# A macaron block with a sorted mixture of experts: each row block is loaded and transposed once and kept, and ScalarE copies each tile's operand from the kept block

## The chip, the cores and the metric

The kernel runs on one core of a Trainium2 chip. The metric is the device time of one launch in microseconds (us). Before the change three runs gave 845.37, 845.60 and 845.91 us, median 845.6 us.

## The reference, cut to what matters

The input x has 4 batches of 512 rows of 256 f32 values. The block adds half a mixture of experts, then a causal attention, then half of the same mixture of experts again, each on the layer norm of x:

```python
x = x + 0.5 * _L0_ffn_ref(_layernorm(x), router_w, gate_w, up_w, down_w)
x = x + _L0_attn_ref(_layernorm(x), Wqkv, Wo)
x = x + 0.5 * _L0_ffn_ref(_layernorm(x), router_w, gate_w, up_w, down_w)

# _L0_ffn_ref: E = 16 experts, K = 2 of them for each row, F = 96, D = 256
probs = softmax(x @ router_w)
routing_weights, routing_idx = top_k(probs, 2)   # weights divided by their sum
expert_out = (silu(x @ gate_w[e]) * (x @ up_w[e])) @ down_w[e]
out = sum over a row's two experts of weight * expert_out
```

The attention has 16 query heads and 4 key heads of 128 values, with rotary embedding.

## The kernel before, in words

**Pools and visits.** A mixture of experts is done by sorting. GpSimd (POOL) scatters each token's normalized row twice, once for each of its experts, with indirect DMAs into a DRAM buffer `xs`, where rows stand in the order of their experts. There are four pools: p0 (batch 0) and p1 (batches 1 to 3) for the first mixture, p2 (batches 0 to 2) and p3 (batch 3) for the second. A pool of `nt` row tiles has `nr = 2 nt` sorted blocks of 128 rows: 8 in p0 and p3, 24 in p1 and p2. Since the boundary between two experts may fall inside a block, a block is multiplied with each expert that has rows in it. This gives `ns = nr + 15` visits (the code calls them tiles): 23 in p0 and p3, 39 in p1 and p2, 124 in all. Visit s belongs to expert e = `tab[s]` and to block s - e. The table is worked out on the chip, so an engine that needs e reads it into a register (TENSOR_LOAD).

**A step of a visit.** `steps(n)` runs over the visits of mixture n, and each engine's program is written out by hand in that order, software-pipelined. At the step of visit `at`:
- SP loads the block of a later visit from `xs` (`load_tile`, a ring of 10 places) after a register read, and stores the output of an earlier one in `ys` (`store_tile`).
- TensorE (PE) runs `gate_up(at)` (two 128x192 matmuls, whose stationary operand is the transposed block in `sb_xT`), `tile_transposes(at + 2)` (two 128x128 transposes of a loaded block into one of two PSUM banks), `load_expert(at + 1)` (the register read), `down(at - 2)` (two matmuls with `sb_hT` stationary), `h_transpose(at - 1)`, and whatever work of the routing or of the attention's projection lies beside.
- ScalarE (ACT) runs `silu(at)`, `xt_copy(at + 2)` (PSUM to `sb_xT`, two places) and `h_copy(at - 1)`.
- VectorE (DVE) runs `h(at)` and `evacuate(at - 2)` (PSUM to an output ring; in the first mixture it is scaled by a row weight that was loaded as column 256 of the block). Routing and norms lie beside.

Every block is so loaded and transposed once for each visit, 124 times. What a matmul needs is handed over by semaphores: `xg_in` (a load landed), `xt_ps` (a transpose is in PSUM), `xt_done` (`sb_xT` is written), `h_done`, `ht_done`, `y_ps` and `y_evac` (an output is evacuated).

**Around the stages.** In the first mixture the steps of p1 follow those of p0 without a break, while ScalarE and VectorE also split the attention's weights. The last steps of p1 carry the norm and projections of the attention. In the second mixture the first visits of p2 start inside the end of the attention, and p3's routing is done beside the first 23 steps of p2. The end is the gather of p3's outputs. Line numbers in the trace: `gate_up` and `down` L1698, `tile_transposes` L1757, `h_transpose` L1771, `silu` L930, `xt_copy` L926, `h` L1263, `evacuate` L1270 and L1272.

## Time and profile before

| | |
|---|---|
| median of three runs | 845.6 us |
| the profiled execution | 844.34 us, of it 842.5 us from the first to the last instruction (the span) |
| mean granted clock of TensorE | 0.978 of 2.4 GHz |
| busy: PE, DVE, ACT, POOL | 91%, 76%, 69%, 53% of the span |
| first mixture, first to last visit | 40.5 to 151.1 us |
| second mixture, first to last visit | 725.8 to 816.8 us |

The two mixtures take about 200 us of the span and the attention between them the rest. A visit is marked in the trace by its `silu`. Busy time counts the matrix work, not the waits; the stages with experts are read by stretches between such marks.

### The profile page before, as it was taken

To read this page: it belongs to the slowest core of one execution; us is meant where nothing else is said; L and a number is where in the kernel's file an instruction comes from. 1 tells how busy PE (TensorE), PEld (TensorE's weight loads), DVE (VectorE), ACT (ScalarE), POOL (GpSimd) and SP (SyncE) were. 2 spreads that over 40 slices of the span, in tenths; PEclk is the share of its full clock that TensorE was granted. 3 is DMA by queue.
4 is the path that set the end of the run, shared out by engine and by line. 5 is a ranking of instruction groups with operands and counts; after the bars stand their busy time and mean duration, and the time that the engine had idled before them with its cause. 6 is when DMAs were issued, how large, how long until landed. Compare 5 with 4: busy or idle time off the path is not lost.

```text
span 842.5 us, 16221 instructions
## 1 busy us (share of the span) xinstructions
PE 762.9 (91%) x4584; PEld 657.5 (78%) x4584; DVE 638.0 (76%) x1839; ACT 580.8 (69%) x1534; POOL 444.6 (53%) x382
## 2 busy tenths in 40 slices
PE   3698999799999999999999999999998989999980
PEld 3686788687878888888888888888887768789970
DVE  6565675578898888889988989997889858755572
ACT  2365657787877887878878787788776666556640
POOL 1571605587565775575667456364444783003374
PEclk9799999999999999999999999999999999999995
DMA  9497962121000100000010000000000156257785
GB/s 313 128 356 241 287 182 83 63 32 20 1 1 14 20 14 8 1 14 14 0 15 12 2 1 2 1 2 1 7 2 1 39 181 186 87 153 234 214 248 173
DMA packets 52918, 70.63 MB, mean 84 GB/s; under 512 B 7264, under 2 KB 44640, under 8 KB 52448
## 3 DMA queue, kind: packets, MB, share of 16 engines
q1 hardware_dynamic: 40736, 47.54, 18.1%
q0 software_dynamic: 9216, 16.82, 8.2%
q10 hardware_dynamic: 2880, 5.24, 1.9%
q8 instruction: 40, 0.66, 0.3%
q14 instruction: 46, 0.38, 0.1%
HBM read 42.80 MB, written 26.77 MB: 83 GB/s over the span
## 4 chain that ended last, share of the span: by engine, by line
PE 67%; DVE 8%; issue 8%; POOL 7%; DMA 4%; ACT 2%; SPq 1%; POOLq 0%; DVEq 0%; ACTq 0%
PE ps L1698 56%; PE ps L1904 6%; PE ps L1757 2%; POOL sb_xf L1647 2%; POOL sb_ropeB L1644 2%; DMA sb_wF_raw<-ys,sb_pos 1%; POOL xs L1605 1%; POOL xs L1613 1%; DVE sb_x L1480 1%; DMA sb_wF_raw<-xs 1%; PE ps L1771 1%; DVE sb_prob L1453 1%; PE ps L1718 1%; DVE sb_wF L1460 1%; PE ps L1865 1%
## 5 line engine op out<-in xcount | busy, mean ns | idle before, releaser
L1698 PE MATMUL ps<-sb_wF 128*128 128x512 f32 (+2 forms) x1056 | 260.2, 373 | 6.2 <-DVE sb_wF L1470 4.9
L1698 PEld LDWEIGHTS ps<-sb_wF 128*128 128x128 f32 x1056 | 171.8, 189 | 25.3 <-issue 5.4
L1698 PE MATMUL ps<-sb_wF,sb_wA 128*128 128x512 f32 x576 | 156.4, 407 | 10.6 <-ACT sb_ropeB L1004 10.0
L1644 POOL TENSOR_TENSOR sb_ropeB<-sb_ropeB,sb_sin 128x512 f32<-128x512 f32 x80 | 110.7, 1384 | 104.8 <-ACT sb_ropeB L1004 104.7
L1023 ACT ACTIVATE sb_prob<-sb_prob,sb_nmax 128x128 f32<-128x128 f32 (+3 forms) x256 | 142.1, 559 | 32.9 <-DVE sb_nmax L1453 32.2
L1655 POOL TENSOR_TENSOR sb_wF<-sb_xf,sb_wF 128x384 fp32r<-128x384 f32 (+1 forms) x75 | 82.3, 1105 | 115.2 <-ACT sb_wF L1016 115.0
L1480 DVE SCALAR_TENSOR_TENSOR sb_x<-ps,sb_rinv,sb_x 128x256 f32<-128x256 f32 x256 | 122.5, 479 | 20.1 <-PE ps L1698 8.9
L1698 PEld LDWEIGHTS ps<-sb_wF,sb_wA 128*128 128x128 f32 x576 | 102.9, 190 | 36.9 <-ACT sb_ropeB L1004 18.1
L1032 ACT ACTIVATE sb_wF<-ps 128x512 fp32r<-128x512 f32 x160 | 95.2, 595 | 43.4 <-PE ps L1904 42.8
L1460 DVE TENSOR_TENSOR sb_wF<-ps,sb_wF 128x512 fp32r<-128x512 f32 x160 | 109.2, 683 | 20.5 <-ACT sb_wF L1032 19.2
L1698 PE MATMUL ps<-sb_wA,sb_wF 128*128 128x256 f32 x768 | 115.5, 286 | 3.9 <-DVE sb_x L1480 3.3
L1698 PEld LDWEIGHTS ps<-sb_wA,sb_wF 128*128 128x128 f32 x768 | 104.1, 189 | 15.2 <-issue 8.3
L1647 POOL TENSOR_TENSOR sb_xf<-sb_xf,sb_ropeB 128x512 f32<-128x512 f32 x80 | 104.5, 1306 | 6.3
L1904 PE MATMUL ps<-sb_ident,sb_prob 128*128 128x128 f32 x640 | 94.0, 273 | 2.5 <-DVE sb_LC L1219 1.4
L1904 PEld LDWEIGHTS ps<-sb_ident,sb_prob 128*128 128x128 f32 x640 | 77.3, 140 | 18.4 <-issue 2.3
L1453 DVE CUSTOM_DVE_ANT_1 sb_prob<-ps,sb_wF_mask 128x384 f32<-128x384 f32 (+1 forms) x128 | 77.5, 618 | 9.4 <-PE ps L1698 8.9
L1698 PE MATMUL ps<-sb_wF_raw,sb_hT 96*128 (+1 forms) x248 | 76.4, 389 | 5.6 <-issue 2.5
L1263 DVE TENSOR_TENSOR sb_sg<-sb_sg,ps 128x96 f32<-128x96 f32 x124 | 31.3, 253 | 59.0 <-ACT sb_sg L930 57.9
L1003 ACT ACTIVATE sb_ropeB<-ps 64x512 f32<-64x512 f32 x80 | 47.6, 595 | 26.0 <-DVE sb_xf L1430 24.4
L1430 DVE SCALAR_TENSOR_TENSOR sb_xf<-ps,sb_cos 128x512 f32<-128x512 f32 x80 | 54.8, 685 | 13.4 <-PE ps L1698 6.7
L1635 POOL DMA_INDIRECT sb_x<-ys,sb_pos x32 | 50.8, 1587 | 26.6 <-DMA ys<-sb_wA_raw 20.5
L930 ACT ACTIVATE sb_sg<-ps 128x96 f32<-128x96 f32 x124 | 30.7, 248 | 45.5 <-PE ps L1698 45.4
(177 smaller groups left out, 1263.1 us busy)
## 6 DMA issues: line engine op xcount, KB each, us to landing
ys<-sb_wA_raw SPq DMA_DIRECT2D x124, 128.0 KB, 3.5
sb_wF_raw<-xs SPq DMA_DIRECT2D x44, 128.5 KB, 4.0
sb_wA_raw<-xs SPq DMA_DIRECT2D x44, 128.5 KB, 2.8
sb_work<-xs SPq DMA_DIRECT2D x36, 128.5 KB
sb_wA_raw<-in_wattn ACTq DMA_DIRECT2D x18, 256.0 KB, 4.4
sb_wF_raw<-in_wgu SPq DMA_DIRECT2D x4, 768.0 KB, 9.8
sb_wF_raw<-in_wdn SPq DMA_DIRECT2D x4, 768.0 KB, 11.6
sb_wA_raw<-in_wgu SPq DMA_DIRECT2D x4, 768.0 KB, 7.6
```

Source lines behind the costliest of these rows:

```text
L1023: nc.scalar.activation(own, own, ACT.Exp, scale=-1.0, bias=nmax[:, k % 2, h:h + 1], accum_out=ssum[:, k % 2, h:h + 1]).then_inc(exp_done, 1)
L1032: nc.scalar.activation(pT_at(tb, 0), ps[:, TBANK + tb % 2], ACT.Copy).then_inc(pt_hi, 1)
L1430: nc.vector.scalar_tensor_tensor(xf[:, rope_slot(col)], ps[:, bank], 1.0 if col == KCOL else SCALE, cos[:], ALU.mult, ALU.mult).then_inc(p ...
L1453: nc.vector.tensor_tensor_reduce(masked, scores, added, 1.0, TOP, ALU.add, ALU.min, nmax[:, k % 2, h:h + 1]).then_inc(nmax_done, 1)
L1460: nc.vector.tensor_tensor(pT_at(tb, 1), ps[:, TBANK + tb % 2], pT_at(tb, 0).bitcast(F32), ALU.subtract).then_inc(pt_lo, 1)
L1480: nc.vector.scalar_tensor_tensor(x[:, b, i], ps[:, wo_bank(b, k, h // 2), at:at + D], rinv[:, k % 4, h:h + 1], x[:, b, i], ALU.mult, ALU.a ...
L1635: nc.gpsimd.indirect_dma_start(out=x[:, t // T, t % T], out_offset=None, in_=ys[q.p][:], in_offset=where, compute_op=ALU.add).then_inc(acc ...
L1644: nc.gpsimd.tensor_tensor(ropeB[:, slot], ropeB[:, slot], sin[:], ALU.mult).then_inc(rope_mul, 1)
L1647: nc.gpsimd.tensor_tensor(xf[:, slot], xf[:, slot], ropeB[:, slot], ALU.add).then_inc(rope_sum, 1)
L1655: nc.gpsimd.tensor_tensor(lo[:, part], xf[:, rope_slot(col), part], hi[:, part].bitcast(F32), ALU.subtract)\
L1698: return nc.tensor.matmul(out, lhsT, rhs, start=start, stop=stop)
L1904: ins = nc.tensor.transpose(ps[:, TBANK + tb % 2, h * P:(h + 1) * P], prob[k % 2][:, h, j * P:(j + 1) * P], ident[:])
```

## The change

Each sorted block is loaded once by `load_block` (64 loads in place of 124; in the second mixture without the weight column, 256 in place of 257 values a row), into a ring of 6 places, and SP no longer reads a register. PE transposes it once (`turn`) into the same two PSUM banks. VectorE copies it from there into a kept region (`keep`; in the first mixture with a second copy of 128x1 for the weight column); only the first two blocks of p2 are kept by ScalarE, in the end of the attention. The semaphore `xt_kept` counts kept blocks. For each visit ScalarE copies the operand from the kept block into a ring of five places of `sb_xT` (`visit` takes the place of `xt_copy`). The block's address comes from a table that SP lays into one row by DMA (`table_row`) and that ScalarE reads four values at a time into registers. `turn(t)` waits until blocks up to t - 2 are kept, since they share the bank.

In mixture n = 0 each pool now runs its own steps from -2 to ns + 1, so p0 is finished before p1 begins. Block i + 4 is turned at step i and kept at step i + 1, so turns stand in steps 0 to 3 of p0, 0 to 19 of p1 and 0 to 19 of p2; p3's blocks are turned at steps 35 to 42 counted from p2's first. Query heads of a group are stored in reverse order, the DMA of a mask is issued later by SP, and the scatter waits for `xt_ps` to reach the new count of transposes.

```diff
+    TAB, TURNED = max(q.ns for q in pools), 5
...
-        xT = sb("xT", [P, 2, K * P], F32, own)
+        xT = sb("xT", [P, TURNED, D + 1], F32, own)
...
-    RING, XR, FR, GR = 8, 10, 4, 16
+    RING, XR, FR, GR = 8, 6, 4, 16
...
+    STARTS = {-2: (0, 1), -1: (2, 3)}, {0: (2, 3), 1: (4, 5)}
+    KEEPS = {-2: (0, 1), -1: (2, 3)}, {0: (2, 3), 2: (4, 5)}
+
+    def turned_blocks(q, at):
+        i = at - q.tiles if q.n == 0 else at - pools[2].tiles
+        out = [(q if q.n == 0 else pools[2], r) for r in STARTS[q.n].get(i, ())]
+        if q.n == 0 and 0 <= i and i + 4 < q.nr:
+            out.append((q, i + 4))
+        elif q.n == 1 and 2 <= i and i + 4 < pools[2].nr:
+            out.append((pools[2], i + 4))
+        elif q.n == 1 and 0 <= at + 4 - pools[3].tiles < pools[3].nr:
+            out.append((pools[3], at + 4 - pools[3].tiles))
+        return out
+
+    def kept_blocks(q, at):
+        i = at - q.tiles if q.n == 0 else at - pools[2].tiles
+        out = [(q if q.n == 0 else pools[2], r) for r in KEEPS[q.n].get(i, ())]
+        if q.n == 0 and 1 <= i and i + 3 < q.nr:
+            out.append((q, i + 3))
+        elif q.n == 1 and 3 <= i and i + 3 < pools[2].nr:
+            out.append((pools[2], i + 3))
+        elif q.n == 1 and 0 <= at + 3 - pools[3].tiles < pools[3].nr:
+            out.append((pools[3], at + 3 - pools[3].tiles))
+        return out
...
-        def load_tile(q, s):
...
+        def table_row(q):
+            sp.wait_ge(tab_done, q.p + 1)
+            sp.dma_start(row_tab[0:1, q.p % 2 * TAB:q.p % 2 * TAB + q.ns],
+                         tab[0:q.ns, q.p:q.p + 1]).then_inc(row_tab_in[q.p], 16)
+
+        def load_block(q, r):
+            t = q.at + r
+            if r == 0:
                 sp.wait_ge(scattered[q.p], 16 * q.nt * (1 if q.n == 0 else 2))
...
+            if t >= XR:
+                sp.wait_ge(xt_kept, t - XR + 1)
+            width = RW if q.n == 0 else D
+            sp.dma_start(block_rows(t)[:, 0:width], xs[q.p][r * P:(r + 1) * P, 0:width]).then_inc(xg_in[t % XR], 16)
...
-        def xt_copy(s):
-            act.wait_ge(xt_ps, s + 1)
-            nc.scalar.activation(xT[:, s % 2], x_at(s), ACT.Copy).then_inc(xt_done, 1)
...
+        def visit(q, s):
...
+            at = s - q.tiles
+            if at == 0:
+                act.wait_ge(row_tab_in[q.p], 16)
+            if at % 4 == 0:
+                more = min(4, q.ns - at)
+                own = row_tab[0:1, q.p % 2 * TAB + at:q.p % 2 * TAB + at + more]
...
+            act.wait_ge(xt_kept, q.at + min(at, q.nr - 1) + 1)
+            if s >= TURNED:
+                act.wait_ge(y_evac, s - TURNED + 1)
+            block = block_of_visit(q, at, visited[at % 4])
+            width = D + 1 if q.n == 0 else D
+            nc.scalar.activation(xT[:, s % TURNED, 0:width], block, ACT.Copy).then_inc(xt_done, 1)
...
-            nc.vector.tensor_scalar(yo(s), y_at(s), tile_at(q, s)[:, D:D + 1], None, ALU.mult).then_inc(y_evac, 1)
+            nc.vector.tensor_scalar(yo(s), y_at(s), xT[:, s % TURNED, D:D + 1], None, ALU.mult).then_inc(y_evac, 1)
+
+        def keep(q, r):
+            t = q.at + r
+            dve.wait_ge(xt_ps, t + 1)
+            ins = nc.vector.tensor_copy(kept_block(q, r, D), x_at(t))
+            if q.n == 0:
+                ins = nc.vector.tensor_copy(kept_block(q, r, RW)[:, D:RW], block_rows(t)[:, D:RW])
+            ins.then_inc(xt_kept, 1)
...
-                if has_tile(n, at - 2):
+                if has_tile(q, at - 2):
                     evacuate(pool_of(at - 2), at - 2)
-                if n == 0 and split_at(at - 1) is not None:
+                if not (q.p == 2 and i <= 2):
+                    for block in kept_blocks(q, at):
+                        keep(*block)
+                if n == 0 and has_tile(q, at) and split_at(at - 1) is not None:
                     weights_low(split_at(at - 1))
...
-        def tile_transposes(q, s):
-            pe.wait_ge(xg_in[s % XR], loaded(s))
+        def turn(q, r):
+            t = q.at + r
+            pe.wait_ge(xg_in[t % XR], loaded(t))
+            if t >= 2:
+                pe.wait_ge(xt_kept, t if t == pools[2].at + AHEAD else t - 1)
             for k in range(K):
-                ins = nc.tensor.transpose(x_at(s)[:, k * P:(k + 1) * P], tile_at(q, s)[:, k * P:(k + 1) * P], ident[:])
+                ins = nc.tensor.transpose(x_at(t)[:, k * P:(k + 1) * P], block_rows(t)[:, k * P:(k + 1) * P], ident[:])
             ins.then_inc(xt_ps, 1)
...
-                if has_tile(n, at + 2) and (n == 0 or i + 2 >= AHEAD or q.p == 3):
-                    tile_transposes(pool_of(at + 2), at + 2)
-                if has_tile(n, at) and has_tile(n, at + 1):
+                for block in turned_blocks(q, at):
+                    turn(*block)
+                if has_tile(q, at) and at + 1 < pools[2 * n + 1].end:
                     load_expert(at + 1)
```

PE, a step in the middle of p2, before: the second matmul of `gate_up`, the two transposes, the register read, `down` and `h_transpose` (an ISA row is the weight load with a register address that belongs to the matmul behind it).

```order
L1698 ISA
L1698 MATMUL ps<-sb_wA_raw,sb_xT 128x192
L1757 MATMUL ps<-sb_ident,sb_work 128x128 [waits xg_in9]
L1757 MATMUL ps<-sb_ident,sb_work 128x128
L1750 TENSOR_LOAD sb_tab
L1698 ISA [waits y_evac,ht_done]
L1698 MATMUL ps<-sb_wF_raw,sb_hT 128x256
L1771 MATMUL ps<-sb_ident,sb_sg 96x128 [waits h_done]
```

The same place after the change:

```order
L1817 ISA
L1817 MATMUL ps<-sb_wA_raw,sb_xT 128x192
L1879 MATMUL ps<-sb_ident,sb_work 128x128 [waits xt_kept,xg_in0]
L1879 MATMUL ps<-sb_ident,sb_work 128x128
L1869 TENSOR_LOAD sb_tab
L1817 ISA [waits y_evac,ht_done]
L1817 MATMUL ps<-sb_wF_raw,sb_hT 128x256
L1893 MATMUL ps<-sb_ident,sb_sg 96x128 [waits h_done]
```

The order is as it was, but the transpose now also waits on `xt_kept`, and behind it wait the register read, `down` and `h_transpose`. This stands in each step with a turn; in the other steps the two transposes are gone.

DVE, steps at the start of p2 while x is normalized beside them (L1153), before: `h`, `evacuate`, then other work.

```order
L1263 TENSOR_TENSOR sb_sg<-sb_sg,ps 128x96 [waits silu_done,stat_step]
L1270 COPY sb_wA_raw<-ps 128x256 [waits y_out0,y_ps]
L1153 TENSOR_SCALAR sb_wA_raw<-sb_x,sb_fmvO,sb_frsO 128x256 [waits wo_done]
L1153 TENSOR_SCALAR sb_wA_raw<-sb_x,sb_fmvO,sb_frsO 128x256
L1263 TENSOR_TENSOR sb_sg<-sb_sg,ps 128x96 [waits silu_done]
```

After the change the norm is L1258 and `keep` is L1382:

```order
L1368 TENSOR_TENSOR sb_sg<-sb_sg,ps 128x96 [waits silu_done]
L1375 COPY sb_wA_raw<-ps 128x256 [waits y_out1,y_ps]
L1382 COPY sb_wA_raw<-ps 128x256 [waits xt_ps]
L1258 TENSOR_SCALAR sb_wF_raw<-sb_x,sb_fmvO,sb_frsO 128x256 [waits wo_done]
L1258 TENSOR_SCALAR sb_wF_raw<-sb_x,sb_fmvO,sb_frsO 128x256
```

The copy into the kept region has come in behind `evacuate`, which itself waits on PE for `y_ps`.

ACT, the end of the attention and the first visit of p2, before: the last `xt_copy` of the two early blocks (L926), the load of the table of functions with a first use, and `silu`.

```order
L1038 ACTIVATE sb_wF<-ps 128x512 [waits wo_done,pv_done]
L926 ACTIVATE sb_xT<-ps 128x256 [waits xt_ps]
L1057 ACT_TABLE_LOAD
L1057 ACTIVATE sb_spare<-sb_exponent 128x1
L930 ACTIVATE sb_sg<-ps 128x96 [waits gu_done]
```

After the change:

```order
L1143 ACTIVATE sb_wF<-ps 128x512 [waits wo_done,pv_done]
L1030 ACTIVATE sb_wA_raw<-ps 128x256 [waits xt_ps]
L1162 ACT_TABLE_LOAD
L1162 ACTIVATE sb_spare<-sb_exponent 128x1
L1015 TENSOR_LOAD sb_row_tab [waits row_tab_in2]
L1025 ISA [waits y_evac,xt_kept]
L1025 ACTIVATE sb_xT<-sb_wA_raw 128x256
```

What was the operand's copy is now the `keep` of block 1 (L1030), and the operand of visit 0 is copied behind the load of the table, a register read and a wait.

## Rows read from the trace of the kernel before

**Rows 1.** The page: busy time, share of the span and instructions of each engine.
```profile
PE 762.9 (91%) x4584; PEld 657.5 (78%) x4584; DVE 638.0 (76%) x1839; ACT 580.8 (69%) x1534; POOL 444.6 (53%) x382
```

**Rows 2.** Windows of silu: stretch, length, busy (visits), PE clock, DMA share, GB/s.
```profile
77.87:111.72 33.85, 4.84 (x20) 1.00 0.96 269
111.72:151.30 39.58, 4.73 (x19) 1.00 0.36 108
725.80:732.05 6.25, 0.98 (x4) 1.00 0.07 22
732.05:758.78 26.73, 4.00 (x16) 1.00 0.53 158
758.78:785.73 26.95, 4.75 (x19) 1.00 0.75 226
785.73:817.10 31.37, 5.75 (x23) 1.00 0.82 241
```

**Rows 3.** Timeline, one plain step of p2: start us, us, engine, line, operation.
```profile
747.76 0.63 PEld L1698 LDWEIGHTS ps<-sb_wA_raw,sb_xT 128*128 128x128 f32 x4
...
747.87 0.81 PE L1698 MATMUL ps<-sb_wA_raw,sb_xT 128*128 x4
747.96 0.42 DVE L1270 COPY sb_wA_raw<-ps 128x256 f32<-128x256 f32 x1
...
748.30 0.26 DVE L1167 MAX8 sb_lgO<-ps 128x8 f32<-128x16 f32 x2
748.36 0.30 PEld L1757 LDWEIGHTS ps<-sb_ident,sb_work 128*128 128x128 f32 x2
...
748.63 0.30 PEld L1698 LDWEIGHTS ps<-sb_wF_raw,sb_hT 96*128 96x128 f32 x2
...
748.74 0.60 PE L1698 MATMUL ps<-sb_wF_raw,sb_hT 96*128 x2
...
748.96 0.12 PEld L1771 LDWEIGHTS ps<-sb_ident,sb_sg 128*96 128x96 f32 x1
```

**Rows 4.** Timeline of DVE in p1: an evacuation and the next operation.
```profile
96.68 0.48 DVE L1272 TENSOR_SCALAR sb_wA_raw<-ps,sb_wF_raw 128x256 f32<-128x256 f32 x1
...
97.08 0.68 DVE L1259 TENSOR_TENSOR sb_wA<-sb_wA_raw,sb_wA 128x512 fp32r<-128x512 f32 x1
```

**Rows 5.** Timeline of DVE: an operation on one column.
```profile
764.08 0.15 DVE L1245 TENSOR_SCALAR sb_tab<-sb_cntO 128x1 int32<-128x1 f32 x1
```

**Rows 6.** Timeline of DVE and the weight loads: end of h to its transpose.
```profile
729.32 0.23 DVE L1263 TENSOR_TENSOR sb_sg<-sb_sg,ps 128x96 f32<-128x96 f32 x1
...
729.61 0.12 PEld L1771 LDWEIGHTS ps<-sb_ident,sb_sg 128*96 128x96 f32 x1 [0.75 <-DVE sb_sg L1263]
```

**Rows 7.** Weight loads, start of p1: transposes that waited, and the next load.
```profile
74.31 0.20 PEld L1757 LDWEIGHTS ps<-sb_ident,sb_wF_raw 128*128 128x128 f32 x2 [1.82 <-DMA sb_wF_raw<-xs]
74.53 0.30 PEld L1698 LDWEIGHTS ps<-sb_wF_raw,sb_hT 96*128 96x128 f32 x2
...
78.72 0.20 PEld L1757 LDWEIGHTS ps<-sb_ident,sb_wF_raw 128*128 128x128 f32 x2 [1.15 <-DMA sb_wF_raw<-xs]
79.30 0.30 PEld L1698 LDWEIGHTS ps<-sb_wF_raw,sb_hT 96*128 96x128 f32 x2 [0.37 <-issue]
```

**Rows 8.** Timeline of PE, last two visits: from one h_transpose to the next.
```profile
815.79 0.27 PE L1771 MATMUL ps<-sb_ident,sb_sg 128*96 128x128 f32 x1
...
817.05 0.28 PE L1771 MATMUL ps<-sb_ident,sb_sg 128*96 128x128 f32 x1
```

**Rows 9.** Timeline, start of p2: first gate_up, table load, first silu.
```profile
724.12 0.63 PEld L1698 LDWEIGHTS ps<-sb_wA_raw,sb_xT 128*128 128x128 f32 x4
...
724.42 1.28 ACT L1057 ACT_TABLE_LOAD   x1
...
725.82 0.23 ACT L930 ACTIVATE sb_sg<-ps 128x96 f32<-128x96 f32 x1
```

**Rows 10.** Chain of work, 60 to 75 us: landing of the last scatter.
```profile
67.17 4.82 DMA xs<-sb_wF_raw,sb_toO
```

More of the change, by code:

```diff
@@ L34, in __init__ @@
         self.ns = self.nr + z.E - 1
-        self.end = tiles + self.ns
+        self.end, self.left = tiles + self.ns, at + self.nr
 class Sizes:
@@ L67, in program @@
         pools.append(Pool(z, len(pools), n, b0, b1, before.end if before else 0,
[L68 removed]
+                          before.halves + before.nh if before else 0, before.left if before else 0))
     MT = max(q.nt for q in pools)
     NFIRST = pools[1].end
+    TAB, TURNED = max(q.ns for q in pools), 5
     def sb(name, shape, dt, at=ctx):
@@ L207, in program @@
     xg_in = [sem(f"xg_in{r}") for r in range(XR)]
+    row_tab_in = [sem(f"row_tab_in{p}") for p in range(4)]
     xt_ps = sem("xt_ps")
+    xt_kept = sem("xt_kept")
     xt_done = sem("xt_done")
@@ L718, in steps @@
         first, second = pools[2 * n:2 * n + 2]
+        if n == 0:
+            for q in (first, second):
+                for i in range(-2, q.ns + 2):
+                    yield q, i, q.tiles + i
+            return
         for i in range(-2, first.ns + second.ns + 2):
@@ L826, in mask, with first_tiles, last_tiles @@
             sp.dma_start(mask_slots(n), A["mask"]).then_inc(mask_in[n], 16)
-        def tiles(first, second, then, at):
-            loads = [(first, s) for s in range(first.ns)] + [(second, s) for s in range(second.ns)]
-            out = 0
-            for m, (q, s) in enumerate(loads):
-                if m == at:
-                    then()
-                due = first.ns - RING if m == first.ns else m - XR + 1
-                while out < due:
-                    store_tile(*loads[out])
-                    out += 1
-                load_tile(q, s)
-            while out < len(loads):
-                store_tile(*loads[out])
-                out += 1
+        def first_tiles():
+            early, late = pools[0:2]
+            for r in range(early.nr):
+                load_block(early, r)
+            for i in range(2, early.ns + 2):
+                if i == 6:
+                    table_row(late)
+                store_tile(early, i - 2)
+                if i == early.ns - RING + 1:
+                    for r in range(XR):
+                        load_block(late, r)
+            for i in range(-2, late.ns + 2):
+                if i >= 2:
+                    store_tile(late, i - 2)
+                for q, r in kept_blocks(late, late.tiles + i):
+                    if r + XR < late.nr:
+                        load_block(late, r + XR)
+                if i == late.nr + E - 4:
+                    sp.wait_ge(xt_done, late.tiles + late.nr + E - 5)
+                    mask(0)
+        def last_tiles(then):
+            early, late = pools[2:4]
+            blocks = [(early, r) for r in range(early.nr)] + [(late, r) for r in range(late.nr)]
+            for r in range(XR):
+                load_block(early, r)
+            n = XR
+            for i in range(late.end - early.tiles + 2):
+                if i >= 2:
+                    q = pool_of(early.tiles + i - 2)
+                    store_tile(q, early.tiles + i - 2 - q.tiles)
+                if i == XR:
+                    then()
+                elif i == early.ns - 12:
+                    table_row(late)
+                while n < len(blocks) and n < i + 3 + XR and (n < early.nr or i >= early.ns - 10 + n - early.nr):
+                    load_block(*blocks[n])
+                    n += 1
         for b in range(B):
@@ L922, in gap_tanh @@
             nc.scalar.activation(gap(q, 1), gap(q, 0), ACT.Tanh, scale=-0.5).then_inc(gtanh_done, 1)
-        def xt_copy(s):
-            act.wait_ge(xt_ps, s + 1)
-            nc.scalar.activation(xT[:, s % 2], x_at(s), ACT.Copy).then_inc(xt_done, 1)
+        visited = {}
+        def visit(q, s):
[5 more added lines that the diff above has]
+                own = row_tab[0:1, q.p % 2 * TAB + at:q.p % 2 * TAB + at + more]
+                _, values = nc.values_load_multi_w_load_instructions(
+                    own, engines=[mybir.EngineType.Activation], min_val=max(at - q.nr + 1, 0),
+                    max_val=min(at + more - 1, E - 1),
+                    skip_runtime_bounds_check_because="an expert's first visit comes after its number of visits")
+                visited.update(enumerate(values))
+            act.wait_ge(xt_kept, q.at + min(at, q.nr - 1) + 1)
[6 more added lines that the diff above has]
+            t = q.at + r
+            act.wait_ge(xt_ps, t + 1)
+            nc.scalar.activation(kept_block(q, r, D), x_at(t), ACT.Copy).then_inc(xt_kept, 1)
         def silu(s):
@@ L1584, in scatter @@
                 pool.wait_ge(to_done, q.p + 1)
-                pool.wait_ge(xt_ps, NFIRST)
+                pool.wait_ge(xt_ps, pools[1].left)
                 pool.wait_ge(xn_done[q.p], q.nt)
```

99 lines of the change are left out of this document (54 added, 45 removed).

## The prediction

> **What bounds the kernel now.** I read the page first. TensorE is busy for 91% of the span and no other engine for more than 76% [rows 1], so a change that takes work off TensorE can pay and one that makes it wait can cost. The page's shares are a mean over stages, and the change touches only the two mixtures, so next I cut both into stretches between the `silu` of chosen visits [rows 2]. The reader is to see how long a visit takes in each: 26.95 / 19 = 1.418 us in the middle of the second mixture, with the clock at 1.00 throughout. From visit 4 to 20 of p2 it is 26.73 / 16 = 1.67, since p3's routing lies beside. In the first 20 visits of p1 it is 33.85 / 20 = 1.69, with the DMA share at 0.96 there.
>
> The timeline of one plain step says what the 1.418 us are [rows 3]. TensorE's weight loads follow each other without a gap: `gate_up` takes its place from 747.76 to 748.36 (0.60), the transposes to 748.63 (0.27), `down` to 748.96 (0.33), and `h_transpose` the rest of the step, 0.21. So a plain step is bound by TensorE itself, and removing 0.27 of it would be worth 0.27, if nothing else came to bind. In p1 something else binds already: transposes stand idle for 1.82 and 1.15 us until their load has landed [rows 7]. These are the two things that the change aims at.
>
> **What it removes.** Sixty of 124 pairs of transposes go, and 60 loads. A step without a turn can't be 1.418 - 0.27 = 1.15 us, because a ring is left that needs no transpose: `h_transpose`, `h_copy`, `down`, `h_transpose`. The last two visits of p3, which have no transposes before either, show its period: 817.05 - 815.79 = 1.26 [rows 8]. With a register read on ScalarE in every fourth step I take 1.30, a gain of 0.12.
>
> **What it adds: a wait in each step with a turn.** `turn` of block i + 4 waits until block i + 2 is kept, and that `keep` stands on VectorE one step earlier behind `evacuate(i - 3)`, which waits for `down(i - 3)`. So TensorE waits in step i for its own `down` of step i - 1, and for two copies on VectorE. I follow the ring once, from the weight load of `down`:
> - load to the end of its last matmul: 748.74 + 0.60 - 748.63 = 0.71 [rows 3];
> - to the start of the evacuation: 0.03 (the `down` one period earlier ended at 749.34 - 1.41 = 747.93, the evacuation began at 747.96) [rows 3];
> - evacuation to the next operation: 748.30 - 747.96 = 0.34 [rows 3]. In the first mixture it is 97.08 - 96.68 = 0.40 [rows 4];
> - `keep`: the same shape and source as that evacuation, so 0.42 to its end [rows 3]. In the first mixture it is 0.34 to the next operation and 0.15 for the weight column, by an operation on one column [rows 5];
> - end on VectorE to the weight load that waits: 729.61 - (729.32 + 0.23) = 0.06 [rows 6];
> - the transposes until `down` can load: 0.27 [rows 3].
>
> That is 1.83 us, and 1.96 in the first mixture, against 1.418. TensorE's own way from `down` to the next turn is shorter: 0.33 + 0.21 + 0.60 = 1.14 against 1.56 to the turn in the ring. So the turn comes 0.42 late, and everything queued behind it on TensorE (register read, `down`, `h_transpose`, the next `gate_up`) is late with it; `evacuate` then waits for that `down`, and the ring repeats. Nothing covers it: the wait lies on the engine that bounds the stage.
>
> Behind the turn stands the register read of the next expert. After a turn that waited, the next weight load came 79.30 - 78.72 = 0.58 us later in one place, and 74.53 - 74.31 = 0.22 in another [rows 7], where 0.27 is usual [rows 3]. So a read that could run ahead in the queue's shadow may be laid open for 0 to 0.31 us. I take 0.12, between the ends and nearer to nothing, as the wait of 0.42 is shorter than those of 1.15 and 1.82. A step with a turn is then 1.95, and 2.08 in the first mixture. The Trainium skill ("DMA: Bandwidth & Descriptors", section "Latency and other measured facts") gives `tensor_load` a floor of about 600 ns. The 0.58 above agrees with it, the 0.22 doesn't; by the page alone each turn would lay open the upper end, which is the third rival below.
>
> **First mixture.** p0 is finished before p1 starts, and p1 can't start before its rows are scattered. The last scatter was issued at 67.17 and took 4.82 to land [rows 10]; nothing of the change shortens it surely, though there is less traffic. The first turn was at 74.31 [rows 7]. From it I count turn 0.48, `keep` 0.57, register read 0.5 and copy 0.4 on ScalarE (estimates from the 0.58 and 0.42 above), and `gate_up` to its end 747.87 + 0.81 - 747.76 = 0.92 [rows 3]: `silu` at 77.2 to 77.3 in place of 77.9, so -0.6 (bounds 0 and -3, should the landing take half as long). Then 20 intervals up to visit 20: two without a `down` of about 1.05 and 18 of 2.08 make 39.5, against 33.85 with its late loads: **+5.7**. The late loads go, but what replaces them is longer. Of the visits after that, six are plain (-0.7); the rest take 39.58 / 19 = 2.08 already, under the attention's projections [rows 2], and I give them nothing. Sum: +4.4.
>
> **Second mixture.** Before, the operand of visit 0 was in place ahead of the table load, and `gate_up(0)` began at 724.12 [rows 9]. Now the operand is copied behind that load, which ends at 724.42 + 1.28 = 725.70, its first use (0.1), a register read (0.5) and the copy (0.4): 726.8, and since the attention's last projection is queued behind `gate_up(0)`, all moves by **+2.7**. At step 2 the block to be kept stands behind that step's own `h`: `gate_up` 0.92, `silu` 0.23 [rows 9], `h` 0.23 [rows 6], `keep` 0.42, three handovers of 0.05, then turn 0.27, `down` 0.33 and `h_transpose` 0.21, in all 2.76 in place of 1.42: **+1.3**. In visits 4 to 20 the ring holds for 16 steps. They would be 16 x 1.95 = 31.2 if all of the routing on TensorE fitted into the waits (+4.5), and 26.73 + 16 x 0.53 = 35.2 if none did (+8.5). That work comes in lumps and a wait holds 0.42, so I take **+7.0**. Fifteen steps without a turn give **-1.8**, p3's eight blocks at steps 35 to 42 cost 8 x 0.53 = **+4.2**, and 18 steps behind them give **-2.2**. Sum: +11.2. The gathers at the end and the attention between the mixtures keep their length, and move.
>
> **Sum.** 4.4 + 11.2 = +15.6 on the profiled 844.34, so 859.9. The median of the runs lies 1.3 above the profiled execution, so I predict **861 us**.
>
> **The rivals.**
> 1. *Faster: the keep is never late.* If VectorE ended the `keep` before TensorE ended the next `gate_up`, a step with a turn would stay at 1.418, p1's stalls would go (20 x 1.418 - 33.85 = -5.5), and -0.6, -0.7, +2.7, -1.8 and -2.2 would stay: -8.1, so 837.5 on the median. It speaks for it that VectorE is free for a fourth of the span [rows 1]. From the end of `down`'s matmul TensorE needs 0.21 + 0.60 less the 0.38 by which that end is behind the weight loads, so 0.43; VectorE needs 0.03 + 0.34 + 0.42 + 0.06 = 0.85. It decides when the copy to be waited for doesn't stand behind the evacuation. I see nothing that puts it ahead.
> 2. *Half: only the first mixture is late.* VectorE's part is 0.13 shorter in the second, and more work lies on TensorE beside the turns there, which may absorb the waits. Then the second mixture adds 2.7 + 1.3 - 1.8 - 2.2 = 0, and the sum is +4.4: 850.
> 3. *The register read is laid open in full.* About 42 turns wait (18 in p1, 16 of p2, 8 of p3), each for 0.19 more than I took: +8.0, so 869. The read of 0.58 speaks for it, that of 0.22 against it. The page of the Trainium skill named above would give this case.
> 4. *No change:* the waits in steps with turns and the gains in p1's loads and in plain steps cancel. It needs a ring of 1.55 or so; the rows leave no room for it.
>
> **How the numbers follow.** My case as summed has a chance of 0.62 (its own range 853 to 867: the routing's bounds -2.5 and +1.5, the landing -2.4, the read -5.0 without any opening, and what a start of a pool may be off, 2), the laid-open read 0.14, half 0.11, faster 0.09, no change 0.04. The range of 849 to 876 takes in half of the ring's waits at its lower end and the third rival at its upper end, and leaves out the faster case, no change and what lies above 876, together about 0.18. A measurement of this kernel can tell 0.2%, 1.7 us, from no change. Faster by more than that: 0.09. Within: 0.04. Slower: 0.87.
>
> **What would show it.** In the profile after, p1 from visit 2 to 20 should run at about 2.1 us a visit and p2 from visit 4 to 20 at about 2.1 to 2.2, with the turn's weight load idle before each transpose for 0.3 to 0.6 and VectorE's `keep` as its releaser, in place of DMA. Steps 20 to 34 of p2 should be near 1.3. ScalarE's first copy of p2 should end near 726.8 less what p1 shifts. The DMA share in p1 should fall well below 0.96. I am wrong if turns start without a wait, if steps without a turn stay at 1.42, or if ScalarE, which now has a copy from SBUF and register reads, becomes the engine that others wait for: then `gate_up` and not the turn would be late.

## The result, and the profile after

The changed kernel takes 879.48 us (median of 4 runs, 878.95 to 880.45) against 845.49 for the kernel before (843.9 to 845.91): a ratio of 1.0415, with a 95% interval of 1.0403 to 1.0428 (the two medians themselves divide to 1.0402). It is 34.0 us slower; 15.6 us were forecast, and 879.48 lies above the range. The profiled execution has a span of 878.4 us, 35.9 more than before.

The page of the kernel after, span and busy time of each engine [rows 1]:

```profile
span 878.4 us, 16007 instructions
...
PE 774.4 (88%) x4464; PEld 645.1 (73%) x4464; DVE 658.5 (75%) x1933; ACT 579.5 (66%) x1536; POOL 443.8 (51%) x382
```

TensorE has 120 matmuls fewer and its share fell from 91% to 88%, that of the weight loads from 78% to 73%: the work went, and waiting came. The windows of `silu` say where (kernel after; columns as in [rows 2]: stretch, length, busy and count of `silu`, clock, DMA share, GB/s):

```profile
80.40:124.97 44.57, 4.86 (x20) 1.00 0.66 167
124.97:164.30 39.33, 4.70 (x19) 1.00 0.20 67
741.58:752.68 11.10, 0.98 (x4) 0.87 0.18 53
752.68:789.24 36.56, 4.00 (x16) 0.99 0.35 108
789.24:816.68 27.44, 4.74 (x19) 1.00 0.52 167
816.68:852.90 36.22, 5.69 (x23) 1.00 0.50 147
```

These are p1's visits 0 to 20 and the rest of p1, then p2's visits 0 to 4, 4 to 20, 20 to 39 (p3's first), and the last 23. Against [rows 2] the first stretch went from 33.85 to 44.57 (+10.7), the start of p2 from 6.25 to 11.10 (+4.9), its next 16 visits from 26.73 to 36.56 (+9.8), the next 19 from 26.95 to 27.44 and the last from 31.37 to 36.22 (+4.9). The rest is p1's first `silu`, 80.42 in place of 77.90, and 2.8 more between the last `silu` of p1 and the first of p2 (577.53 in place of 574.77). The DMA share in p1 fell from 0.96 to 0.66, as the halved loads should make it, and the stretch is longer all the same.

One step with a turn in p2, timeline of the kernel after (start us, us, engine, line, operation, idle before and releaser):

```profile
774.92 0.42 DVE L1375 COPY sb_wA_raw<-ps 128x256 f32<-128x256 f32 x1 [0.49 <-PE ps L1817]
...
775.26 0.41 DVE L1382 COPY sb_wA_raw<-ps 128x256 f32<-128x256 f32 x1
...
775.79 0.20 PEld L1879 LDWEIGHTS ps<-sb_ident,sb_work 128*128 128x128 f32 x2 [0.44 <-issue]
775.82 0.41 PE L1879 MATMUL ps<-sb_ident,sb_work 128*128 128x128 f32 x2 [0.18 <-DVE sb_wA_raw L1382]
...
776.42 0.30 PEld L1817 LDWEIGHTS ps<-sb_wF_raw,sb_hT 96*128 96x128 f32 x2 [0.42 <-issue]
776.42 0.69 PE L1817 MATMUL ps<-sb_wF_raw,sb_hT 96*128 x2 [0.19 <-issue]
...
777.16 0.42 DVE L1375 COPY sb_wA_raw<-ps 128x256 f32<-128x256 f32 x1 [0.84 <-PE ps L1817]
```

The ring of the prediction can be read off. `evacuate` at 774.92, the `keep` 0.34 later, its end at 775.67, the turn's weight load at 775.79, `down` at 776.42, its last matmul ends at 777.11, and the next `evacuate` starts at 777.16. The period is 777.16 - 774.92 = 2.24 us against 1.95 forecast. Evacuation (0.34), `keep` (0.41) and `down` (0.69 and 0.05) are as forecast from [rows 3]. Two terms are not: 0.12 from the copy's end to the turn in place of 0.06, and 0.63 from the turn to `down`, where 0.39 was taken (0.27 for the transposes and 0.12 for the register read behind them).

The steps without a turn were to take 1.30. Many take 1.26 to 1.27, but around each fourth visit one or two are longer; in the last 18 intervals the pattern is 1.27, 1.26, 1.83, 1.74. Timeline of the kernel after, ScalarE in the last 18 visits, and the weight load that waits for it:

```profile
826.98 0.25 ACT L1034 ACTIVATE sb_sg<-ps 128x96 f32<-128x96 f32 x1 [0.38 <-PE ps L1817]
...
827.14 0.42 ACT L1025 ACTIVATE sb_xT<-sb_wF_raw 128x256 f32 x1
...
827.59 0.27 ACT L1040 ACTIVATE sb_hT<-ps 96x128 f32<-96x128 f32 x1
...
828.24 0.25 ACT L1034 ACTIVATE sb_sg<-ps 128x96 f32<-128x96 f32 x1 [0.38 <-PE ps L1817]
...
829.59 0.42 ACT L1025 ACTIVATE sb_xT<-sb_wF_raw 128x256 f32 x1 [1.10 <-DVE sb_wA_raw L1375]
...
829.91 0.25 ACT L1040 ACTIVATE sb_hT<-ps 96x128 f32<-96x128 f32 x1
...
830.31 0.19 PEld L1817 LDWEIGHTS ps<-sb_wF_raw,sb_hT 96*128 96x128 f32 x1 [1.14 <-issue]
```

`silu`, the copy of an operand and `h_copy` follow each other from 826.98 on, and the next `silu` comes 1.26 later. Then, at 828.49, ScalarE stands for 1.10 us before the next copy. In this step it reads four values of the table. The trace names an evacuation as releaser, but that one (it began at 828.74 and took 0.42) had ended at 829.16. `h_copy` is behind the copy and comes late, so `down` waits 1.14.

### The profile page after: what moved, and what is told of

It is laid out like the page before. It is cut to its first block, busy times and chain, and to the rows that moved or that the text cites. A ratio compares the mean times of both kernels' runs of the same rounds, so it can differ in the third digit from the quotient of the medians.

```text
span 878.4 us, 16007 instructions
## 1 busy us (share of the span) xinstructions
PE 774.4 (88%) x4464; PEld 645.1 (73%) x4464; DVE 658.5 (75%) x1933; ACT 579.5 (66%) x1536; POOL 443.8 (51%) x382
## 4 chain that ended last, share of the span: by engine, by line
PE 57%; issue 14%; DVE 12%; POOL 8%; ACT 3%; DMA 2%; ACTq 1%; POOLq 0%; DVEq 0%
PE ps L1817 47%; PE ps L2026 5%; POOL xs L1710 2%; PE ps L1879 2%; POOL sb_xf L1766 2%; POOL sb_ropeB L1763 2%; DVE sb_wA_raw L1377 1%; DMA sb_wF_raw<-ys,sb_pos 1%; DVE sb_wF_raw L1382 1%; POOL sb_wF L1774 1%; DVE sb_wA_raw L1375 1%; DVE sb_prob L1572 1%; DVE sb_x L1599 1%; PE ps L1837 1%; DVE sb_wF L1579 1%
## 5 line engine op out<-in xcount | busy, mean ns | idle before, releaser
L1817 PE MATMUL ps<-sb_wF,sb_wA 128*128 128x512 f32 x576 | 156.3, 407 | 10.7 <-ACT sb_ropeB L1109 10.0
L1817 PEld LDWEIGHTS ps<-sb_wF,sb_wA 128*128 128x128 f32 x576 | 102.8, 190 | 37.1 <-ACT sb_ropeB L1109 18.4
L1817 PE MATMUL ps<-sb_wF_raw,sb_hT 96*128 (+1 forms) x248 | 84.2, 421 | 20.2 <-ACT sb_hT L1040 9.1
L1817 PEld LDWEIGHTS ps<-sb_wF_raw,sb_hT 96*128 96x128 f32 x248 | 37.7, 190 | 41.9 <-issue 36.2
L1040 ACT ACTIVATE sb_hT<-ps 96x128 f32<-96x128 f32 x124 | 33.3, 269 | 44.4 <-PE ps L1893 43.3
```

Source lines behind the costliest of these rows:

```text
L1817: return nc.tensor.matmul(out, lhsT, rhs, start=start, stop=stop)
```

## The experiments

All times are medians, and each ratio is to runs of the kernel before on the same chip; each edit is against the changed kernel, or against the experiment that is named. The kernel before had a median of 846.28 beside experiments 1 to 4, 844.72 beside 5 to 8 and 844.48 beside 9 to 11, so a difference between times of different groups, or to the 879.48 above, is good to about 2 us.

**1. The keep ahead of the evacuation.** On VectorE, save in p2's first three steps:

```diff
+                if not (q.p == 2 and i <= 2):
+                    for block in kept_blocks(q, at):
+                        keep(*block)
                 if has_tile(q, at):
                     h(at)
...
                     evacuate(pool_of(at - 2), at - 2)
-                if not (q.p == 2 and i <= 2):
-                    for block in kept_blocks(q, at):
-                        keep(*block)
```

> VectorE's keep is moved ahead of h and of the evacuation in its step (not in the first three steps of p2). Theory of the ring (the turn is late because the keep it needs stands behind the evacuation, which waits for down): the keep no longer waits for down, so the turn finds its block kept and the register read behind it runs ahead again. Steps with a turn go from 2.36 (p1) and 2.24 (p2) to about 1.45; p1's first 20 steps from 42.3 to about 29.5 us, p2's visits 4 to 20 from 36.6 to about 27, p3's eight turns from 15.9 to about 11.5; the time falls by about 27 to 852. Rival (it is VectorE's added work, some 0.5 us a step, that is too much beside the evacuation and h, wherever it stands): the steps stay above 2.1 and the time above 872.

Measured: 855.12 us, 1.0093 times the kernel before (1.0073 to 1.0114). Windows of `silu` of this run, p1's visits 0 to 20 and p2's 4 to 20:

```profile
79.06:112.18 33.12, 4.87 (x20) 1.00 0.85 230
738.80:767.01 28.21, 4.02 (x16) 1.00 0.48 145
```

44.57 became 33.12 and 36.56 became 28.21. Not all that was expected came: p1's stretch was to be 29.5, and p3's eight turns took 13.13 where 11.5 was expected. The same number of instructions in another order on one engine gives back 24.4 of the 34 us. So the greater part was not VectorE's work but the place of the copy.

**2. The register read ahead of the turn.** On TensorE:

```diff
+                if has_tile(q, at) and at + 1 < pools[2 * n + 1].end:
+                    load_expert(at + 1)
                 for block in turned_blocks(q, at):
                     turn(*block)
-                if has_tile(q, at) and at + 1 < pools[2 * n + 1].end:
-                    load_expert(at + 1)
```

> TensorE's register read of the next expert is moved ahead of the turn that waits. Theory of the laid-open read: 0.36 us of each late turn's step is the read that couldn't start before the turn; it now hides under gate_up and the wait. Turn steps go from 2.36 to 2.0 and from 2.24 to 1.88; with 18 in p1, 16 in p2 (part of which lies beside the routing) and 8 for p3 the time falls by 12 to 15, to 865 to 868. Rival (the read is not what TensorE waits for behind the turn): 879.

Measured: 865.98 us, 1.022 (1.0195 to 1.0245), 13.5 less than the changed kernel. TensorE's weight loads in a step with a turn of this run:

```profile
761.96 0.63 PEld L1817 LDWEIGHTS ps<-sb_wA_raw,sb_xT 128*128 128x128 f32 x4
763.03 0.20 PEld L1879 LDWEIGHTS ps<-sb_ident,sb_work 128*128 128x128 f32 x2 [0.44 <-issue]
763.29 0.30 PEld L1817 LDWEIGHTS ps<-sb_wF_raw,sb_hT 96*128 96x128 f32 x2
```

The turn still waits 0.44 (the ring is still there), but `down` now follows 0.26 behind it, where it was 0.63. Steps with a turn took 1.87 here, and 2.00 in p1. That is the ring alone, forecast at 1.83 and 1.96; the difference to 2.24, 0.37, is the read.

**3. The turn at the end of TensorE's step.**

```diff
-                for block in turned_blocks(q, at):
-                    turn(*block)
...
                     h_transpose(at - 1)
+                for block in turned_blocks(q, at):
+                    turn(*block)
                 beside(q, i)
```

> The turn is moved to the end of TensorE's step, behind down and h_transpose. Theory of the ring: the copy that it waits for has 0.8 us more, TensorE's own way from down to the turn becomes 1.95 us against 1.6 needed by the evacuation and the keep, so turns don't wait and nothing but the next gate_up stands behind them: turn steps of about 1.45, time near 852 as with the keep moved. Rival (the copy's work itself is too much for VectorE): no less than 872.

Measured: 854.79 us, 1.009 (1.0067 to 1.0114), the same as the first experiment. The ring may be opened on either of its engines.

**4. ScalarE's reads left out.** The address of an operand is a constant:

```diff
-                _, values = nc.values_load_multi_w_load_instructions(
...
-            block = block_of_visit(q, at, visited[at % 4])
+            block = kept_block(q, at - at * (E - 1) // (q.ns - 1), D + 1 if q.n == 0 else D)
```

> ScalarE's register read of the table is left out: the address of each visit's operand is a constant, so visits may copy another block than their own and the output is not the reference's; the work is the same. Theory of ScalarE's reads: of four steps without a turn one takes 1.8 instead of 1.27 us since the read of four values (about 1.1 us) stands ahead of h_copy. Without it p2's steps 20 to 35 go from 20.5 to 19.1 and the last 18 from 26.9 to 23.0; steps with a turn have room and change little; the time falls by 5 to 8, to 872 to 874. Rival (the long fourth steps come from another wait, as that for the evacuated output): 879.

Measured: 873.02 us, 1.0317 (1.0292 to 1.0341), 6.5 less than the changed kernel. The long steps are gone (the last 18 intervals take 22.74 in place of 26.87), so they were the read and not the evacuation that the trace named.

**5. The pools joined**, on top of the first experiment: `steps(0)` runs from p0 to p1 without a break, as before the change.

```diff
-            for q in (first, second):
-                for i in range(-2, q.ns + 2):
-                    yield q, i, q.tiles + i
-            return
```

> On top of the keep moved ahead: the steps of p1 follow those of p0 without a break again, so p1's first blocks are turned and kept inside p0's last steps. Theory of the drain: p1's first turns stand on TensorE behind all of p0's work (5.5 us between the last silu of p0 and the first of p1), not behind the scatter; joined, the first silu of p1 comes at 75.5 to 76.5 in place of 79.1, and the time falls by about 3 from 855.1 to 852. Rival (the start waits for the landing of p1's scattered rows, as was assumed in the prediction): less than 1 us.

Measured: 856.65 us, 1.0138 (1.0102 to 1.0175), no better than the first experiment. The first `silu` of p1 came at 76.87, 2.2 earlier than there, but visit 20 at 114.33 in place of 112.20. SP's queue and TensorE's weight loads of this run:

```profile
72.75 7.02 SPq L878 DMA_DIRECT2D ys<-sb_wA_raw  x8
...
79.81 0.53 SPq L873 DMA_DIRECT2D sb_work<-xs  x1
...
82.22 0.20 PEld L1884 LDWEIGHTS ps<-sb_ident,sb_work 128*128 128x128 f32 x2 [2.85 <-DMA sb_work<-xs]
```

The turn of p1's block 6 waited 2.85 for a load that SP issued at 79.81, behind eight stores of p0's last visits. This wait is shown; that it is the whole reason is not. So the theory of the drain failed as a gain: what is won ahead of p1's first visit is lost at its fourth.

**6. One read in each step**, on top of the first experiment: ScalarE reads the next visit's value alone, behind `h_copy`.

```diff
                     h_copy(at - 1)
+                if has_tile(q, at + 2) and has_tile(q, at + 3) and at + 3 > pool_of(at + 3).tiles:
+                    look_up(pool_of(at + 3), at + 3 - pool_of(at + 3).tiles)
```

> On top of the keep moved ahead: ScalarE reads one value of the table in each step, behind h_copy, for the next visit, in place of four in every fourth step ahead of a visit. Theory of ScalarE's reads: one read of four leaves ScalarE still for 1.1 us and h_copy late by 0.5; ScalarE is idle for 0.38 between h_copy and silu, so a single read hides there or adds at most 0.1. The long fourth steps go: p2's steps 20 to 35 from 20.6 to 19.2-20.5, the last 18 from 26.9 to 23-25, p1's first 20 from 33.1 to about 29; time 845 to 850 against 855.1. Rival (a read costs as much alone as four together, about 1.1 us): each step is longer by 0.6, the time over 880.

Measured: 845.92 us, 1.0015 (0.9999 to 1.0031): 9.2 less than the first experiment, level with the kernel before. ScalarE's timeline in the last visits of this run, then windows of `silu` for p1's visits 0 to 20, p2's 20 to 35 and the last 18:

```profile
800.80 0.27 ACT L1040 ACTIVATE sb_hT<-ps 96x128 f32<-96x128 f32 x1
801.45 0.25 ACT L1034 ACTIVATE sb_sg<-ps 128x96 f32<-128x96 f32 x1 [0.38 <-PE ps L1819]
801.62 0.42 ACT L1025 ACTIVATE sb_xT<-sb_wF_raw 128x256 f32 x1
802.06 0.27 ACT L1040 ACTIVATE sb_hT<-ps 96x128 f32<-96x128 f32 x1
```

```profile
76.55:109.84 33.29, 4.84 (x20) 1.00 0.88 241
...
764.24:783.79 19.55, 3.75 (x15) 1.00 0.50 162
795.11:818.00 22.89, 4.63 (x19) 1.00 0.70 197
```

A read between `h_copy` (800.80) and `silu` (801.45) doesn't lengthen the step of 1.26. All of the last visits now take that, 22.75 us from the first `silu` of that stretch to the last in place of 25.34 before the change: here is the gain that the change was to bring. In p1 it did not come: its first 20 visits, expected at about 29, took 33.29.

**7. No reads on ScalarE**, as in the fourth experiment, on top of the first.

```diff
-            block = block_of_visit(q, at, visited[at % 4])
+            block = kept_block(q, at - at * (E - 1) // (q.ns - 1), D + 1 if q.n == 0 else D)
```

> On top of the keep moved ahead: ScalarE's reads are left out (constants for the address, so an operand may come from another block than its own, and the output is not the reference's). It gives the bound of what ScalarE's reads cost once the turns don't wait: p1's 20 steps 28.5 to 29.5, p2's steps 20 to 35 19.1, the last 18 22.8, time about 845 to 847, that is level with the kernel before. Rival (the kernel is held by something else by then, such as the start of p2): above 850.

Measured: 846.61 us, 1.0014 (0.9998 to 1.0029), the same as with one read a step. So single reads in that place cost nothing that can be measured.

**8. Joined pools and single reads**: the edits of the first, fifth and sixth experiments together, of which the lines are these.

```diff
-            for q in (first, second):
-                for i in range(-2, q.ns + 2):
...
+                    look_up(pool_of(at + 3), at + 3 - pool_of(at + 3).tiles)
```

> Keep moved ahead, joined pools and single reads together. If the three causes are separate their gains add: 855.1 less 3 less 5 to 10, so 842 to 847. If the projections at p1's end hide what p1 gains, 847 to 850.

Measured: 850.16 us, 1.0059 (1.0032 to 1.0086), slower than the single reads alone. In its profile the turn of block 6 waited 3.09 us behind eight stores on SP, as in the fifth.

**9. The keeps ahead in p2's start too**, on top of the sixth.

```diff
-    KEEPS = {-2: (0, 1), -1: (2, 3)}, {0: (2, 3), 2: (4, 5)}
+    KEEPS = {-2: (0, 1), -1: (2, 3)}, {0: (2, 3), 1: (4, 5)}
...
+                for block in kept_blocks(q, at):
+                    keep(*block)
                 if q.p == 2 and i == 0:
                     x_add(B - 1, UB - 1, 0)
```

> On top of the keep moved ahead and single reads: in p2's first steps too the keeps stand ahead, blocks 2 and 3 ahead of the additions and h of step 0, blocks 4 and 5 in step 1 ahead of its h. Theory of the start: what is left of the loss is p2's start, where visit 2 and the turn of block 6 wait for keeps behind h, additions and norm statistics on VectorE (11.4 us for visits 0 to 4 in place of 6.3, part of it at half clock after TensorE stood idle). They fall to 7.5 to 9 us, and the time by 2.5 to 4 from 845.9, to 842 to 843.5, below the kernel before (844.7 in that comparison). Rival (visit 2's wait is for the attention's last projection): less than 1 us.

Measured: 845.82 us, 1.0011 (0.9996 to 1.0026). The stretch went as expected in the profile (visits 0 to 4 from 11.40 to 8.15), the time didn't. In the profiled execution, one of the longer ones of a spread from 842.67 to 847.89, the turn of p1's block 6 waited 3.61 us, against 1.54 in the profile of the sixth:

```profile
81.70 0.23 PEld L1877 LDWEIGHTS ps<-sb_ident,sb_work 128*128 128x128 f32 x2 [3.61 <-DMA sb_work<-xs]
```

The tenth, whose p1 is the same, waited 0.64 there, so this wait changes from one execution to the next. Whether it accounts for the whole of the missing gain is open: these are single profiles.

**10. The first two visits of p2 ahead of the table load**, on top of the ninth.

```diff
                     visit(pool_of(at + 2), at + 2)
+                if q.p == 2 and i == -1:
+                    nc.scalar.activation(spare[:, 1:2], exponent[:, 0:1], ACT.Silu)
...
                 elif what == "silu":
-                    nc.scalar.activation(spare[:, 1:2], exponent[:, 0:1], ACT.Silu)
+                    pass
```

> As the run before, and the first two visits of p2 are copied on ScalarE ahead of the load of the table of functions, not behind it. Theory of the first visit: gate_up of visit 0 starts 1.4 us earlier, the attention's last projection with it, and the first silu waits for the table load again; 1 to 1.5 us less than the run before. Rival (the first silu, now behind the load, holds VectorE's chain): no gain.

Measured: 842.78 us, 0.9979 (0.9965 to 0.9992): less than the kernel before by about 2 us (0.2%, by an interval that narrowly leaves out 1), and 3.0 less than the ninth. Windows of `silu`, p2's visits 0 to 4 and 4 to 20:

```profile
723.83:731.34 7.51, 0.98 (x4) 1.00 0.20 57
731.34:759.71 28.37, 4.00 (x16) 1.00 0.48 145
```

**11. The same with joined pools**, and with SP's loads of p1's blocks 6 to 9 between p0's last stores.

```diff
                 store_tile(early, i - 2)
...
+                for q, r in kept_blocks(late, early.tiles + i) if i >= early.ns - 2 else ():
+                    load_block(late, r + XR)
```

> As the run before, with p0 and p1 joined and SP's loads of p1's blocks 6 to 9 put between the stores of p0's last visits. Theory of the queue on SP: joining the pools gained nothing before because p1's block 6 stood behind eight stores on SP (a turn waited 2.9 us for it); freed of that, p1's visit 20 comes 1.5 to 3 us earlier and the time falls by as much. Rival (p1's blocks can't be there earlier, since scatter and loads share the DMA engines): within 1 us of the run before.

Measured: 842.39 us, 0.9976 (0.9965 to 0.9986), the same as the tenth. The theory fails: the wait for block 6 is gone, but visit 20 of p1 came no earlier (111.85, against 110.13 in the tenth). TensorE, now with p1's turns among p0's last visits, waits for the load of p1's first block instead, as the rival would have it:

```profile
72.90 0.29 PEld L1886 LDWEIGHTS ps<-sb_ident,sb_work 128*128 128x128 f32 x2 [3.84 <-DMA sb_work<-xs]
```

## Why the prediction was wrong

The direction and the main cause stood. The turn waits for a `keep` that stands behind the evacuation, and that behind `down`; the second experiment measured this ring without anything else at 1.87 where 1.83 was worked out, and moving the copy or the turn took the waits away. The sum was too small by 18.4 us. These are the steps that failed:

- **"I take 0.12, between the ends and nearer to nothing"**, for the register read behind the turn. It was laid open in full: 0.63 from the turn to `down` where it is 0.26 with the read ahead, so 0.37 in each late turn that a read follows, above the upper end of 0.31 too. Taking it away is worth 13.5 us; 42 x 0.12 = 5.0 were in the sum. The error lay in how [rows 7] were read. The transposes at 74.31, with the next load 0.22 later, are those of p1's first visit, in the step that would read the expert of p0's last visit. The bounds in `expert_of` coincide for the first and the last visit of a pool (0 and 0, 15 and 15), and the program has no register read for them. So the 0.22 was no fast read: there was none. In p1's first 20 visits four transposes with a read behind them waited for their load, for 0.48 to 1.15 us, and the next weight load came 0.58 (at 78.72, [rows 7]) to 1.19 us later, the longer ones perhaps with other waits in them. Weight loads of the kernel before, one of them; then of the kernel after at the end of p2, a late turn in a step without a read:

```profile
83.83 0.20 PEld L1757 LDWEIGHTS ps<-sb_ident,sb_work 128*128 128x128 f32 x2 [0.53 <-DMA sb_work<-xs]
84.61 0.30 PEld L1698 LDWEIGHTS ps<-sb_wF_raw,sb_hT 96*128 96x128 f32 x2 [0.58 <-issue]
...
813.07 0.20 PEld L1879 LDWEIGHTS ps<-sb_ident,sb_xf 128*128 128x128 f32 x2 [0.44 <-issue]
813.33 0.30 PEld L1817 LDWEIGHTS ps<-sb_wF_raw,sb_hT 96*128 96x128 f32 x2
```

This turn waited the same 0.44 as the one at 775.79, and `down` followed 0.26 behind it. So the choice by the length of the wait had no ground, and the third rival, with the read laid open each time, was this case and had too low a chance. The Trainium skill ("DMA: Bandwidth & Descriptors", section "Latency and other measured facts") gives `tensor_load` a floor of about 600 ns. The trace agrees in size: 0.63 lies between the weight loads of a late turn and of `down`, with the transposes and the read in it.

- **"With a register read on ScalarE in every fourth step I take 1.30"**. The read of four values holds ScalarE for 1.10 us ahead of `h_copy`, and a group of four steps takes 1.27 + 1.26 + 1.83 + 1.74 = 6.1, so 1.53 a step, longer than the 1.418 before. The last 18 intervals, forecast to gain 2.2, lost 1.5. It is felt in p0 too: p1 started 2.5 late in the changed kernel, and 0.7 to 1.7 early with the reads out or alone and the pools apart (the fourth, sixth, seventh, ninth and tenth), where the sum had it 0.6 early. The start isn't the reads' alone: with the turn last and the reads in (the third) p1 started 0.1 early. In all 6.5 us by the fourth experiment, against 1.3 allowed (33 steps of 0.04).
- **"At step 2 the block to be kept stands behind that step's own `h`: ... +1.3"**. Start and first four visits of p2 together lost 2.76 + 4.85 = 7.6, with 4.0 forecast; the start alone came as forecast (+2.7). What I left out is the other work on VectorE in those steps. Timeline of the kernel after, a copy of ScalarE in step 0 of p2, then step 2, VectorE and the weight load:

```profile
744.48 0.42 ACT L1025 ACTIVATE sb_xT<-sb_wA_raw 128x256 f32 x1 [2.63 <-DVE sb_wA_raw L1382]
...
746.54 0.74 DVE L1212 BATCH_NORM_STATS2 sb_fstatsO<-sb_x 128x6 f32<-128x256 f32 x2
747.20 0.24 DVE L1368 TENSOR_TENSOR sb_sg<-sb_sg,ps 128x96 f32<-128x96 f32 x1
747.36 0.74 DVE L1382 COPY sb_wA_raw<-ps 128x256 f32<-128x256 f32 x2
747.89 0.20 PEld L1879 LDWEIGHTS ps<-sb_ident,sb_work 128*128 128x128 f32 x2 [1.95 <-issue]
```

In step 0 the copy for visit 2 waits 2.63 for the `keep` of block 2, which stands behind additions and `h`; the next `silu` is behind that copy, and the first interval is 3.20 in place of 1.75. In step 2 the statistics of the norm stand ahead of `h`, and this ahead of the `keep` of blocks 4 and 5. The turn that needs block 4 waits 1.95 us, where the forecast's chain leaves 1.35 (0.92 + 0.23 + 0.23 + 0.42 + 0.15 from the start of `gate_up` to the end of the `keep`, less 0.60 for `gate_up`'s weight loads). The interval from visit 3 to 4, 2.77 in place of 1.41, fell to a lower clock, of which the last section has more.

These three excesses are 8.5, 5.2 and 3.6 us, together 17.3 of the 18.4. Since they are measured in different runs, the split is good to a few us. The remainder holds the 0.06 a turn of the longer handover, and 0.5 of the 0.7 us that p1's later visits were to gain. By stretches of the profile the excess is 3.1 at p1's start, 5.0 in its first 20 visits, 3.6 at p2's start, 2.8 from its visit 4 to 20 and 3.7 in the last 18 intervals; the rest is 1.1 or less each.

Right were the late loads of p1 going without a gain, steps without a turn at 1.26 where no read stood in the way, p3's eight turns (15.91 - 11.32 = +4.6, forecast +4.2), and the first rival's condition: "when the copy to be waited for doesn't stand behind the evacuation". With it met (experiment 1) the steps with turns are at 1.42 again where ScalarE's reads don't lengthen them, and with single reads (experiment 6) p3's eight turns take 11.32 as before the change. That alone didn't make the kernel faster. The rival had no more for ScalarE's reads than the sum had and nothing for the late `keep`s at p2's start, and the 5.5 us that it gives to p1's first 20 visits didn't come: 33.12 in experiment 1 against 33.85.

What stays open is p1's start and its first 20 visits. In the profiles of experiments 1 to 10 the turn of block 6 waited between 0.4 and 3.6 us, each time for a load that SP issues behind eight stores; in the eleventh that wait is gone, and the one of 3.84 for the first block is there. A larger ring of loaded blocks wasn't tried. From 84 to 110 us no turn of the sixth waits for a load, and p1 is still no faster than before: `down` waits there in six places, 3.1 us in all, for something that the profile doesn't name.

## What to carry to other kernels

Before work is moved to another engine, write down the ring that the new semaphore closes, with every instruction ahead of the one that signals: a copy that nobody needs early, put behind one that waits, cost 0.8 us in a step of p2 with a late turn, with the read behind it (2.24 against 1.42). A register read behind the instruction that waits added 0.37 us to the step; put it ahead, or into a gap of the engine, and don't put four in a row where a gap holds one. Before a row is taken for the price of an instruction, see that the instruction is there. Sixty loads and sixty pairs of transposes saved were worth 2 us in the end, and only after four places had been put right: the order of the copies, the reads, and two in p2's start.

## What the runs showed of the hardware

**A wait is paid twice when the clock falls after it.** Windows of the kernel after at p2's start (stretch, length, busy time of PE, PEld, DVE, ACT, POOL, then granted clock, DMA share, GB/s):

```profile
746.00:748.00 2.00, 0.32 (x3) 0.11 (x2) 2.00 (x8) 0.34 (x2) 0.00 (x0) 1.00 0.19 53
...
749.50:751.00 1.50, 1.50 (x8) 1.17 (x7) 0.78 (x7) 0.61 (x3) 0.00 (x0) 0.58 0.26 87
751.00:753.00 2.00, 2.00 (x9) 1.90 (x8) 0.82 (x3) 0.57 (x3) 0.88 (x1) 0.50 0.43 131
```

TensorE was busy for 0.32 of 2.0 us and for 1.38 of the next 1.50, where the clock was still 1.00. It ran all through the two stretches after that, and there the granted clock was 0.58 and 0.50 of full speed; 0.50 is the lower level of 1.2 GHz. It does not follow each such wait. In the first experiment the same turn waited 1.95 us as well and the clock stayed:

```profile
734.00:736.00 2.00, 0.48 (x3) 0.30 (x3) 1.60 (x6) 0.44 (x2) 0.00 (x0) 1.00 0.00 0
736.00:738.00 2.00, 2.00 (x13) 1.75 (x14) 1.32 (x8) 0.85 (x3) 0.00 (x0) 1.00 0.03 10
```

Its interval from visit 3 to 4 took 1.41. In the sixth, with the same order on VectorE, the clock was 0.70 and 0.50 from 732 to 736 us behind that wait, and the interval took 2.63 (2.77 in the kernel after), so the fall cost some 1.2 us there. The clock fell in the ninth run too, behind the wait for block 6:

```profile
80.00:82.00 2.00, 0.29 (x2) 0.23 (x2) 0.00 (x0) 0.00 (x0) 0.00 (x0) 0.96 0.74 225
82.00:84.00 2.00, 2.00 (x7) 1.55 (x6) 0.59 (x2) 0.32 (x2) 1.62 (x1) 0.50 0.17 58
...
86.00:88.00 2.00, 2.00 (x15) 1.76 (x13) 2.00 (x7) 1.39 (x5) 1.68 (x2) 1.00 1.04 282
```

Seven matmuls ran from 82 to 84 us, at the lower level; from 86 to 88 us, at clock 1.00, it was fifteen. I had counted waits at their own length only.

**Reads of registers differ by their place more than by their number.** One in each step, in a gap of 0.38 us between `h_copy` and `silu`, cost nothing that can be measured in 33 steps; four in one step held ScalarE for 1.10 us. On TensorE one read behind a late turn added 0.37 us, and ahead of the turn nothing that shows.
